# The queries' row factor: from two TensorE transposes a pair to a block turn on VectorE and a way through DRAM

## The chip, the cores and the metric

The kernel runs on one core of one Trainium2 chip. The metric is the device time of one execution in microseconds. TensorE (PE, with its weight loads PEld), VectorE (DVE), ScalarE (ACT), GpSimd (POOL) and SyncE (SP) each run their own queue of instructions and wait for one another through semaphores.

## The reference

128 sequences of 128 tokens, 256 hidden numbers, 16 heads of 16. A gated cross-attention with an additive bias, then a gated mixture of 8 experts of which each token takes one:

```python
x = x + tanh(g_xattn) * attention(layernorm(x), ctx, ctx, bias, Wq.., Wk.., Wv..)   # LoRA merged into W
x = x + tanh(g_ffn) * ffn(layernorm(x))       # argmax over 8 experts, gelu, two 256x256 products
# attention: scores = (q * D**-0.5) @ k.T + bias; softmax; out = p @ v
# layernorm(x) = (x - mean) / sqrt(var + 1e-5), one mean and one factor for each row (token)
```

## The kernel before

The attention half runs in steps, one for each sequence: in step k TensorE multiplies the scores of sequence k, while earlier and later sequences stand at other stages (`seq(i, k, lag)` gives the sequence that is lag steps back; a negative lag is ahead). Eight steps make one round of a hardware loop on each engine. The order inside a step is written out by hand for each engine. Queries and keys are projected for two sequences at once: in an even step the queries of a pair (`qry`, two sequences ahead), in an odd step its keys (`ky`, one ahead). The expert half follows; the change does not touch it.

The layernorm of the queries is folded into the projection: the weights are centred, so that only the factor 1/sqrt(var+eps) of each token is missing. It is a column: one number on each of 128 partitions, in `ln[:, row, 0, 0]`, made by GpSimd (L486) five steps ahead of the sequence's scores. The projected queries lie with the hidden numbers on the partitions and the tokens along the free axis, so the factor is needed as a row, the same on all partitions: `RS`, 128 x 256 for a pair.

One even step on TensorE runs thus (the lines are those of the profile): scores of k (L575), for which it waits that x2T of the step before was read (L638), scaled_ok and others; the values product of k-2 (L609); the first eight transposes of the scores of k-1 (L600); four transposes of the output (L676); then the two transposes of the row factor (L707), each with `ln`'s column broadcast along the free axis, into the unused half of bank 6; the query projection (L625, eight matmuls); the value projection (L735) into the other half of bank 6, after a wait that ScalarE has copied the row factor out; two transposes of the normalised rows (L749) into bank 3; the last eight transposes of the scores of k-1 (L600). Then the next step's scores, which overwrite banks 0 to 3. An odd step has the key projection in place of the query projection and no row factor. Every fourth step adds the expert logits (L648, L679), the next one the count sums (L685, L686).

ScalarE in a step: copy of the logits (L885, every fourth step), copy of the output (L870), two exponentials (L876), the second layernorm (L863), in an even step the copy of the row factor out of PSUM (L910), in an odd step the key activations (L853), the copy of V (L917), the copy x2T (L923), two more exponentials (L876), in an even step the bias activations of the queries (L842). VectorE: in every fourth step the picking of experts (L1063 to L1076), in the next the list of slots; 16 additions of the bias with their maximum (L1035); the division by the softmax sums (L1130, L1134), the residual (L1141), in an even step `scale_queries` (L1094), which multiplies the projected queries in PSUM by RS, the statistics for the layernorms (L1045, L1050, L1058). GpSimd subtracts the maxima (L462), makes the factors (L484, L486, L491), adds the value bias (L499) and scatters the normalised rows to DRAM (L519). SyncE issues all loads of the steps; ScalarE's queue issues DMAs only before the steps (weights, L830, L832) and after them (L332).

Of the kernel before, what the change touches and what calls it, by code (L numbers as in the profile page):

```python
# [12 lines left out]
P = 128  # L13
# [85 lines left out]
def flamingo_block(nc, x, x_turned, ctx_in, bias, wqT, wkT, wvT, bv, lora_in,  # L99
                   w1, w2, b2, consts, out):  # L100
    ctx = ExitStack()
    with ctx:
        def sb(name, shape, dt=F32):
            return ctx.enter_context(nc.sbuf_tensor(name, shape, dt))

        def sem(name):
            return ctx.enter_context(nc.semaphore(name))

        rows_dram = nc.dram_tensor("rows_dram", (DUMMY + FT, ROW), F32, kind="Internal").ap()

# [24 lines left out]
        sc = sb("sc", [P, 4, HEADS * P])  # L135
        RS = sb("RS", [P, 2 * P])
        XT = sb("XT", [P, 2, KC, 2 * P])
# [62 lines left out]
        b_x, b_o = bank[6], bank[7]  # L200
        b_v, b_rs, b_x2 = b_x[:, 0:HID], b_x[:, HID:HID + 2 * P], b_s[3]
        o_ps = b_o[:].rearrange("p (h c) -> p h c", c=CELL)
# [49 lines left out]
        xT_in = [sem(f"xT_in{i}") for i in range(2)]  # L252
        rs_ready, rs_evac = sem("rs_ready"), sem("rs_evac")
        s_setc, scaled_ok = sem("s_setc"), sem("scaled_ok")
# [287 lines left out]
        def _(pe):  # L542
# [86 lines left out]
            def step(i, k):  # L629
# [69 lines left out]
                if isinstance(i, int) and k in (N - 2, N - 1):  # L699
                    turn_rows(early[k - N + 2])  # L700
                if qry and qry.slot(2) == 0:
                    pe.wait_ge(rs_ok, qry.n(1, 2))
                    if not cur and val.reached(1):
                        pe.wait_ge(v_evac, val.n())
                    for n in range(2):
                        rs = ln[:, (qry.k + n - 7) % 8, 0, 0:1].broadcast_to([P, P])
                        ins = nc.tensor.transpose(b_rs[:, P * n:P * n + P], rs, ident)  # L707
                    ins.then_inc(rs_ready, 1)
                if cur and (qry or ky):
# [17 lines left out]
                if val:  # L727
                    pair, tok = val.k // 2 % 4, P * val.slot(2)
                    pe.wait_ge(ctx_inn[pair], val.per(8, 16, 16))
                    if qry and qry.slot(2) == 0:  # L730
                        pe.wait_ge(rs_evac, qry.per(2, 1, 1))
                    elif not cur and val.reached(1):
                        pe.wait_ge(v_evac, val.n())
                    for c in range(KC):
                        ins = mm(b_v, CT[:, pair, c, tok:tok + P], W["v"][:, c, :],  # L735
                                 start=(c == 0), stop=(c == KC - 1))
                    ins.then_inc(v_ready, 1)
# [90 lines left out]
        def _(act):  # L828
# [43 lines left out]
            def probs(t, q):  # L872
                act.wait_ge(tr_ready, t.n(4, q + 1))
                if q == 0 and t.reached(2):
                    act.wait_ge(ot_ready, t.n(1, -1))
                nc.scalar.activation(PT[:, t.slot(2), 512 * q:512 * q + 512], turn_bank(t, q)[:],  # L876
                                     ACT.Exp).then_inc(pt_ready, 1)

            def step(i, k):
                val, qry, ky, prev, fin, old, gate = (seq(i, k, lag) for lag in (-3, -2, -1, 1, 2, 3, 4))  # L880
                if gate and gate.slot(4) == 3:
                    act.wait_ge(lt_ready, gate.per(4, 1, 1))
                    if gate.reached(4):
                        act.wait_ge(l_ok, gate.per(4))
                    nc.scalar.copy(LT[:], b_lt).then_inc(lt_evac, 1)  # L885
# [20 lines left out]
                if isinstance(i, int) and k in (N - 2, N - 1):  # L906
                    copy_rows(early[k - N + 2])
                if qry and qry.slot(2) == 0:
                    act.wait_ge(rs_ready, qry.per(2, 1, 1))
                    nc.scalar.copy(RS[:], b_rs).then_inc(rs_evac, 1)  # L910
                if ky and ky.slot(2) == 0:
                    keys(ky)
                if val:
                    act.wait_ge(v_ready, val.n(1, 1))
                    if val.reached(8):
                        act.wait_ge(ot_ready, val.n(1, -7))
                    nc.scalar.copy(V[:, val.slot(8), :, 0:D],  # L917
                                   b_v.rearrange("p (h d) -> p h d", d=D)).then_inc(v_evac, 1)
                if old:
                    act.wait_ge(x2t_ready, old.n(1, 1))  # L920
# [7 lines left out]
                if qry and qry.slot(2) == 0:  # L928
                    queries(qry)

            early = [At(0, k, FU) for k in range(5)]
# [50 lines left out]
        def _(dve):  # L982
# [106 lines left out]
            def scale_queries(t):  # L1089
                pair = t.k // 2 % 2  # L1090
                dve.wait_ge(rs_evac, t.per(2, 1, 1))
                for o in range(KC):
                    dve.wait_ge(q_ready, t.per(2, KC, o + 1))
                    ins = nc.vector.tensor_tensor(QT[:, pair, o, :], b_s[o][:, 0:2 * P], RS[:], ALU.mult)  # L1094
                ins.then_inc(scaled_ok, 1)

            def step(i, k):
                cur, done, gate, ahead = seq(i, k, 0), seq(i, k, 2), seq(i, k, 4), seq(i, k, -5)
                qry = seq(i, k, -2)
                grp, was_grp = seq(i, k, 5), seq(i, k, 6)  # L1100
# [9 lines left out]
                if cur:  # L1110
                    for q in range(4):
                        add_bias(cur, q)
                if here.reached(2) and (gate or done or grp):
                    dve.wait_ge(o_ready, here.n(1, -1))
# [281 lines left out]
```

## Time and profile before

| | us |
|---|---|
| median of 3 runs (lowest, highest) | 1283.41 (1283.16, 1283.64) |
| the profiled execution | 1286.07 |
| its span | 1284.2 |
| attention steps | about the first 970 of the span |

Shares of busy time over the whole span, and the span in 40 slices (each digit the busy share in tenths; the last quarter is the expert half):

```profile
PE 1250.6 (97%) x12696; PEld 1071.5 (83%) x12696; DVE 996.9 (78%) x5961; ACT 781.1 (61%) x1724; POOL 999.9 (78%) x1051
PE   8999999999999999999999999999998799999997
DVE  6778888888888888888888888887897556555654
ACT  2767667677767676777676767776676333333332
POOL 3778889889888888888888888888888544554545
PEclk9999999999999999999999999999999899999999
```

TensorE's matmuls are pipelined, so the time of one in the trace is longer than what it holds of TensorE. A wait of an engine stands in brackets behind the instruction that ended it.

### The profile page before, as it was taken

What the parts mean: (1) busy time and instruction counts of PE and PEld (TensorE: products, weight loads), DVE (VectorE), ACT (ScalarE), POOL (GpSimd) and SP (SyncE); (2) the same over time, 40 slices, a digit from 0 to 9 for tenths busy, and PEclk for the clock granted to TensorE, in tenths of its full rate; (3) what the DMA queues carried; (4) which work ended last, traced back from release to release, by engine and by line L of the source; (5) the groups of instructions that cost most, each with busy time, mean ns of one, the idle gap of its engine ahead of it and who ended that gap; (6) DMA issues with size and microseconds to landing.
All of it is one profiled execution on the core that took longest, in us unless ns stands there. A gap on an engine that the chain in (4) does not pass through costs nothing.

```text
span 1284.2 us, 45363 instructions
## 1 busy us (share of the span) xinstructions
PE 1250.6 (97%) x12696; PEld 1071.5 (83%) x12696; DVE 996.9 (78%) x5961; ACT 781.1 (61%) x1724; POOL 999.9 (78%) x1051
## 2 busy tenths in 40 slices
PE   8999999999999999999999999999998799999997
PEld 6888888888888888888888888887887678888886
DVE  6778888888888888888888888887897556555654
ACT  2767667677767676777676767776676333333332
POOL 3778889889888888888888888888888544554545
PEclk9999999999999999999999999999999899999999
DMA  7656666666666666666666666666666388988885
GB/s 261 221 192 219 215 203 208 207 210 213 201 207 217 212 202 213 209 213 201 209 221 206 210 206 219 203 201 198 204 201 217 120 251 275 283 278 274 284 268 181
DMA packets 119875, 280.34 MB, mean 218 GB/s; under 512 B 16356, under 2 KB 35302, under 8 KB 119680
## 3 DMA queue, kind: packets, MB, share of 16 engines
q1 hardware_dynamic: 106128, 243.55, 59.7%
q0 software_dynamic: 12624, 34.62, 6.9%
q10 hardware_dynamic: 1056, 1.39, 0.4%
q8 instruction: 28, 0.46, 0.2%
q14 instruction: 39, 0.32, 0.1%
HBM read 243.50 MB, written 36.91 MB: 218 GB/s over the span
## 4 chain that ended last, share of the span: by engine, by line
PE 90%; issue 3%; DVE 3%; DMA 1%; POOL 1%; another core or an unknown queue 1%; ACT 1%; POOLq 0%; DVEq 0%; ACTq 0%
PE bank L600 18%; PE bank L625 17%; PE bank L575 11%; PE bank L609 9%; PE bank L735 8%; PE bank L778 8%; PE bank L792 7%; PE bank L676 4%; PE bank L749 2%; PE bank L766 2%; DMA out<-og,ids 1%; PE bank L648 1%; PE bank L707 1%; DVE sc L1035 1%
## 5 line engine op out<-in xcount | busy, mean ns | idle before, releaser
L1035 DVE CUSTOM_DVE_ANT_0 sc<-bank,sc 128x128 f32<-128x128 f32 x2048 | 442.9, 286 | 121.6 <-PE bank L575 109.9
L462 POOL TENSOR_TENSOR sc<-sc,rowmax 128x1024 f32<-128x1024 f32 x256 | 480.3, 1900 | 21.0 <-DVE rowmax L1035 16.7
L876 ACT ACTIVATE PT<-bank 128x512 f32<-128x512 f32 x512 | 279.9, 603 | 2.5 <-PE bank L600 1.8
L600 PE MATMUL bank<-cst,sc 128*128 128x128 f32 x2048 | 272.6, 276 | 0.6 <-POOL sc L462 0.6
L600 PEld LDWEIGHTS bank<-cst,sc 128*128 128x128 f32 x2048 | 225.4, 140 | 26.6 <-issue 25.3
L534 POOL DMA_INDIRECT out<-og,ids x120 | 118.3, 986 | 120.4 <-issue 113.7
L519 POOL DMA_INDIRECT rows_dram<-x2n,slot_i x128 | 135.2, 1056 | 62.1 <-issue 55.8
L1035 DVE DVE_READ_ACCUMULATOR2_ANT rowmax<- 128x1 f32 x2048 | 170.1, 83 | 0.2 <-issue 0.2
L870 ACT COPY OT<-bank 128x512 f32<-128x512 f32 x128 | 75.0, 586 | 134.9 <-PE bank L609 134.9
L575 PE MATMUL bank<-KT,QT 32*128 32x256 f32 x2048 | 146.7, 400 | 3.4 <-ACT V L917 1.2
L609 PE MATMUL bank<-PT,V 128*32 128x128 f32 x4096 | 137.6, 275 | 0.6 <-ACT PT L876 0.6
L853 ACT ACTIVATE KT<-bank,bk_half,cst 128x256 f32<-128x256 f32 x256 | 123.6, 563 | 21.9 <-PE bank L625 20.7
L609 PEld LDWEIGHTS bank<-PT,V 128*32 128x32 f32 x4096 | 106.6, 110 | 32.4 <-ACT PT L876 27.2
L917 ACT COPY V<-bank 128x256 f32<-128x256 f32 x128 | 48.4, 378 | 138.7 <-PE bank L735 138.7
L735 PE MATMUL bank<-wv,CT 128*128 128x256 f32 x512 | 132.3, 381 | 0.0
L792 PE MATMUL bank<-CT,hT 128*128 128x256 f32 x516 | 124.5, 383 | 5.7 <-DVE sc L1257 5.7
L625 PE MATMUL bank<-XT,wq 128*128 128x256 f32 x512 | 124.7, 388 | 4.3 <-DVE rowmax L1035 4.3
L625 PE MATMUL bank<-CT,wk 128*128 128x256 f32 x512 | 123.7, 384 | 0.9 <-DVE rowmax L1035 0.9
L778 PE MATMUL bank<-xgT,w_sb 128*128 128x256 f32 (+1 forms) x552 | 123.0, 366 | 0.0
L575 PEld LDWEIGHTS bank<-KT,QT 32*128 32x128 f32 x2048 | 92.8, 184 | 28.8 <-issue 24.2
L792 PEld LDWEIGHTS bank<-CT,hT 128*128 128x128 f32 x516 | 98.1, 192 | 19.3 <-ACT hT L949 6.1
L735 PEld LDWEIGHTS bank<-wv,CT 128*128 128x128 f32 x512 | 98.0, 191 | 13.6
(151 smaller groups left out, 1964.4 us busy)
## 6 DMA issues: line engine op xcount, KB each, us to landing
sc<-in_bias SPq DMA_DIRECT2D x256, 512.0 KB
w_sb<-in_w SPq DMA_DIRECT2D x69, 257.0 KB
CT<-in_w SPq DMA_DIRECT2D x69, 256.0 KB
xg<-rows_dram SPq DMA_DIRECT2D x63, 272.0 KB
x_sb<-in_x SPq DMA_DIRECT2D x128, 128.0 KB, 2.0
CT<-in_ctx_in SPq DMA_DIRECT2D x64, 256.0 KB, 4.7
XT<-in_x_turned SPq DMA_DIRECT2D x64, 256.0 KB, 2.7
rows_dram<-x2n,slot_i POOLq DMA_INDIRECT x128
```

The lines of the kernel that those rows point to most:

```text
L462: nc.gpsimd.tensor_tensor(s, s, m, ALU.subtract).then_inc(sub_ok, 1)
L519: nc.gpsimd.indirect_dma_start(rows_dram, bass.IndirectOffsetOnAxis(ap=slot_i[:, g, j:j + 1], axis=0), x2n[:, t.slot(8), :], None).then_in ...
L575: ins = mm(b_s[j][:, 2 * P * c:2 * P * c + 2 * P], QT[rows, pair, c, P * sq:P * sq + P], KT[rows, pair, c, sq].rearrange("p e k -> p (e k) ...
L600: ins = nc.tensor.transpose(turn_bank(t, q)[:, P * h:P * h + P], sc[:, t.slot(4), o:o + P], ident)
L609: ins = mm(b_x[CELL * j:CELL * j + CELL, P * (h // 4):P * (h // 4) + P], V[:, t.slot(8), h, :], PT[:, t.slot(2), P * h:P * h + P], start=T ...
L625: ins = mm(b_s[o][:, 0:2 * P], W[w][:, c, o * P:o * P + P], moving[:, c, :], start=(c == 0), stop=(c == KC - 1))
L735: ins = mm(b_v, CT[:, pair, c, tok:tok + P], W["v"][:, c, :], start=(c == 0), stop=(c == KC - 1))
L778: ins = mm(h_bank(t)[:, FT * o:FT * o + P * halves(t)], w1_of(t)[:, c * HID + o * P:c * HID + o * P + P], xgT[:, t.slot(2), c, 0:P * halve ...
L792: ins = mm(y_half, hT[:, t.slot(2), c, a * P:a * P + P], w2_of(t)[:, c * HID:c * HID + HID], start=(c == 0), stop=(c == KC - 1))
L853: ins = nc.scalar.activation(KT[:, pair, o, :, e, :], b_s[o][:, 0:2 * P].rearrange("p (s k) -> p s k", s=2), ACT.Identity, bias=bk_half[:, ...
L876: nc.scalar.activation(PT[:, t.slot(2), 512 * q:512 * q + 512], turn_bank(t, q)[:], ACT.Exp).then_inc(pt_ready, 1)
L1035: ins = nc.vector.tensor_tensor_reduce(out=s, in0=b_s[q][:, P * (h % 4):P * (h % 4) + P], in1=s, scale=1.0, scalar=LOWEST, op0=ALU.add, op ...
```

## The change

TensorE no longer transposes the row factor, ScalarE no longer copies it out of PSUM, and neither waits for the other over it. In their place, for each sequence t in step t-4: VectorE turns `ln`'s column, broadcast to 32 columns, in blocks of 32x32, so that one partition of each strip of 32 holds the 32 factors of its strip as a row (behind the bias additions). ScalarE's queue sends these four rows of 32 numbers to DRAM, 512 bytes (behind the copy of V, ahead of the copy x2T), and at the end of the same step, after a wait that they have landed, loads them back, broadcast to 128 partitions, into RS. RS becomes two buffers, one for each pair in flight. `scale_queries` waits for the loads.

```diff
+        rs_dram = nc.dram_tensor("rs_dram", (N, STRIPS, STRIP), F32, kind="Internal").ap()
-        RS = sb("RS", [P, 2 * P])
+        RS, rs_turned = sb("RS", [P, 2, 2 * P]), sb("rs_turned", [P, 2, STRIP])
 # TensorE, step
-                if qry and qry.slot(2) == 0:
-                    pe.wait_ge(rs_ok, qry.n(1, 2))
-                    if not cur and val.reached(1):
-                        pe.wait_ge(v_evac, val.n())
-                    for n in range(2):
-                        rs = ln[:, (qry.k + n - 7) % 8, 0, 0:1].broadcast_to([P, P])
-                        ins = nc.tensor.transpose(b_rs[:, P * n:P * n + P], rs, ident)
-                    ins.then_inc(rs_ready, 1)
...
-                    if qry and qry.slot(2) == 0:
-                        pe.wait_ge(rs_evac, qry.per(2, 1, 1))
-                    elif not cur and val.reached(1):
+                    if not cur and val.reached(1):
                         pe.wait_ge(v_evac, val.n())
 # ScalarE
+            def send_scale(t):
+                act.wait_ge(rs_turn, t.n(1, 1))
+                act.nop(nofuse=True)
+                act.dma_start(rs_dram[t.n()], rs_turned[0:P:STRIP, t.slot(2), :]).then_inc(rs_out, 16)
+
+            def spread_scale(t):
+                pair, tok = t.k // 2 % 2, P * t.slot(2)
+                act.wait_ge(rs_out, t.n(16, 16))
+                act.nop(nofuse=True)
+                act.dma_start(RS[:, pair, tok:tok + P], rs_dram[t.n()].rearrange("(a b) c -> a (b c)", a=1)
+                              .partition_broadcast(P)).then_inc(rs_in[pair], 16)
 # ScalarE, step
+                behind = seq(i, k, -4)
-                if qry and qry.slot(2) == 0:
-                    act.wait_ge(rs_ready, qry.per(2, 1, 1))
-                    nc.scalar.copy(RS[:], b_rs).then_inc(rs_evac, 1)
                 if ky and ky.slot(2) == 0:
                     keys(ky)
                 if val:
...
                     nc.scalar.copy(V[:, val.slot(8), :, 0:D],
                                    b_v.rearrange("p (h d) -> p h d", d=D)).then_inc(v_evac, 1)
+                if behind:
+                    send_scale(behind)
                 if old:
                     act.wait_ge(x2t_ready, old.n(1, 1))
...
                 if qry and qry.slot(2) == 0:
                     queries(qry)
+                if behind:
+                    spread_scale(behind)
 # VectorE
             def scale_queries(t):
                 pair = t.k // 2 % 2
-                dve.wait_ge(rs_evac, t.per(2, 1, 1))
+                dve.wait_ge(rs_in[pair], t.per(4, 32, 32))
...
-                    ins = nc.vector.tensor_tensor(QT[:, pair, o, :], b_s[o][:, 0:2 * P], RS[:], ALU.mult)
+                    ins = nc.vector.tensor_tensor(QT[:, pair, o, :], b_s[o][:, 0:2 * P], RS[:, pair, :], ALU.mult)
+            def turn_scale(t):
+                dve.wait_ge(rs_ok, t.n(1, 1))
+                if t.reached(2):
+                    dve.wait_ge(rs_out, t.n(16, -16))
+                dve.nop(nofuse=True)
+                nc.vector.transpose(rs_turned[:, t.slot(2), :], ln[:, (t.k - 7) % 8, 0, 0:1].broadcast_to([P, STRIP])
+                                    ).then_inc(rs_turn, 1)
 # VectorE, step
                 if cur:
                     for q in range(4):
                         add_bias(cur, q)
+                if behind:
+                    turn_scale(behind)
                 if here.reached(2) and (gate or done or grp):
                     dve.wait_ge(o_ready, here.n(1, -1))
```

## Rows read from the trace of the kernel before

**Rows 1.** Busy time by engine, 60 to 960 us: window, length, busy (count), clock, DMA.
```profile
60.00:960.00 900.00, 895.47 (x10436) 765.75 (x10434) 762.56 (x5075) 630.62 (x1398) 790.81 (x823) 1.00 0.63 207
```

**Rows 2.** Chain that ended last, two even steps: start us, share us, what.
```profile
507.21 0.24 PE bank L707 x2
...
521.91 0.22 PE bank L707 x2
```

**Rows 3.** Instruction groups by form on VectorE: count, busy us, mean ns, idle before.
```profile
L1035 DVE DVE_READ_ACCUMULATOR2_ANT rowmax<- 128x1 f32 x2048 | 170.1, 83 | 0.2 <-issue 0.2
L1130 DVE RECIPROCAL rden<-bank 128x16 f32<-128x16 f32 x128 | 32.0, 250 | 1.0 <-PE bank L676 1.0
L1124 DVE TENSOR_TENSOR where<-bank,cst 128x32 f32<-128x32 f32 x32 | 6.0, 186 | 1.8 <-PE bank L686 1.4 <-PE bank L690 0.4
```

**Rows 4.** Timeline, end of an even step: start us, length us, engine, line, instruction.
```profile
524.75 0.37 ACT L917 COPY V<-bank 128x256 f32<-128x256 f32 x1 [1.85 <-PE bank L735]
525.02 0.38 ACT L923 COPY x2T<-bank 128x256 f32<-128x256 f32 x1
525.09 0.33 SPq L371 DMA_DIRECT2D XT<-in_x_turned  x1
525.74 0.50 PE L575 MATMUL bank<-KT,QT 32*128 32x256 f32 x4
```

**Rows 5.** Timeline, ends of two odd steps.
```profile
516.67 0.59 PE L735 MATMUL bank<-wv,CT 128*128 128x256 f32 x2
517.39 0.38 ACT L917 COPY V<-bank 128x256 f32<-128x256 f32 x1
517.64 0.41 ACT L923 COPY x2T<-bank 128x256 f32<-128x256 f32 x1
518.29 0.50 PE L575 MATMUL bank<-KT,QT 32*128 32x256 f32 x4
...
533.04 0.41 ACT L923 COPY x2T<-bank 128x256 f32<-128x256 f32 x1
533.63 0.71 PE L575 MATMUL bank<-KT,QT 32*128 32x256 f32 x8
```

**Rows 6.** Timeline, query scaling and next scores: expert-picking step; the one late step.
```profile
540.08 0.74 DVE L1094 TENSOR_TENSOR QT<-bank,RS 128x256 f32<-128x256 f32 x2
541.18 0.50 PE L575 MATMUL bank<-KT,QT 32*128 32x256 f32 x4
...
889.86 0.75 DVE L1094 TENSOR_TENSOR QT<-bank,RS 128x256 f32<-128x256 f32 x2
890.70 1.15 PE L575 MATMUL bank<-KT,QT 32*128 32x256 f32 x16 [0.64 <-issue]
```

**Rows 7.** Single lines, 520-526 and 517-519 us: count, ns min/median/max, start us.
```profile
L922 ACTq EVENT_SEMAPHORE  x1: 17/17/17, 524.8 to 524.8; - x1
...
L571 PEldq EVENT_SEMAPHORE  x1: 438/438/438, 517.7 to 517.7; - x1
```

**Rows 8.** Timeline, DMA issues on SyncE's and ScalarE's queues.
```profile
518.59 0.85 SPq L380 DMA_DIRECT2D sc<-in_bias  x2
...
1021.63 0.58 ACT L939 COPY xgT<-bank 128x512 f32<-128x512 f32 x1
1021.78 0.34 ACTq L332 DMA_DIRECT2D rows_dram<-vacant  x1
```

**Rows 9.** Timeline, the output copy that follows the even step of rows 4.
```profile
528.40 0.59 ACT L870 COPY OT<-bank 128x512 f32<-128x512 f32 x1 [0.54 <-PE bank L609]
```

**Rows 10.** DMA issues: count, KB each, median us from issue to landing.
```profile
x_sb<-in_x SPq DMA_DIRECT2D x128, 128.0 KB, 2.0
CT<-in_ctx_in SPq DMA_DIRECT2D x64, 256.0 KB, 4.7
```

**Rows 11.** Timeline, the start of the kernel.
```profile
12.69 0.37 ACT L917 COPY V<-bank 128x256 f32<-128x256 f32 x1 [7.79 <-PE bank L735]
...
14.97 0.85 DVE L1094 TENSOR_TENSOR QT<-bank,RS 128x256 f32<-128x256 f32 x2
```

More of the change, by code:

```diff
@@ L200, in flamingo_block @@
         b_x, b_o = bank[6], bank[7]
-        b_v, b_rs, b_x2 = b_x[:, 0:HID], b_x[:, HID:HID + 2 * P], b_s[3]
+        b_v, b_x2 = b_x[:, 0:HID], b_s[3]
         o_ps = b_o[:].rearrange("p (h c) -> p h c", c=CELL)
@@ L252, in flamingo_block @@
         xT_in = [sem(f"xT_in{i}") for i in range(2)]
-        rs_ready, rs_evac = sem("rs_ready"), sem("rs_evac")
+        rs_turn, rs_out, rs_in = sem("rs_turn"), sem("rs_out"), [sem(f"rs_in{i}") for i in range(2)]
         s_setc, scaled_ok = sem("s_setc"), sem("scaled_ok")
@@ L1090, in scale_queries @@
                 pair = t.k // 2 % 2
-                dve.wait_ge(rs_evac, t.per(2, 1, 1))
+                dve.wait_ge(rs_in[pair], t.per(4, 32, 32))
                 for o in range(KC):
                     dve.wait_ge(q_ready, t.per(2, KC, o + 1))
-                    ins = nc.vector.tensor_tensor(QT[:, pair, o, :], b_s[o][:, 0:2 * P], RS[:], ALU.mult)
+                    ins = nc.vector.tensor_tensor(QT[:, pair, o, :], b_s[o][:, 0:2 * P], RS[:, pair, :], ALU.mult)
                 ins.then_inc(scaled_ok, 1)
+            def turn_scale(t):
[5 more added lines that the diff above has]
+                                    ).then_inc(rs_turn, 1)
             def step(i, k):
                 cur, done, gate, ahead = seq(i, k, 0), seq(i, k, 2), seq(i, k, 4), seq(i, k, -5)
-                qry = seq(i, k, -2)
+                qry, behind = seq(i, k, -2), seq(i, k, -4)
                 grp, was_grp = seq(i, k, 5), seq(i, k, 6)
```

## Prediction

> **What bounds the kernel now.** I first took the busy times of the long stretch of attention steps: TensorE is busy for 895.5 of 900 us at the full clock, VectorE for 763, GpSimd for 791, ScalarE for 631 [rows 1]. Next I read the chain of work that ended last; in that stretch it runs through TensorE without a break. The pieces that the change removes stand on it as 0.22 and 0.24 us for the two transposes of one pair of sequences, between the transposes of the output and the query projection [rows 2]. I take 0.23 us a pair.
>
> Then I asked what may hold up TensorE if ScalarE gets later, because the change puts new work into ScalarE's queue. The timeline of an even step (queries) and of two odd steps (keys) answers that. At the end of a step TensorE does the value projection (L735), ScalarE copies it (V, L917), then copies the turned rows (x2T, L923), and the next step's scores (L575) wait for x2T (L638: x2T was read out of bank 3, which the scores overwrite). In the even step x2T ends at 525.40 and the scores start at 525.74; in the odd steps 518.05 and 518.29, 533.45 and 533.63 [rows 4, 5]. So x2T comes in 0.18 to 0.34 us ahead. Not all of this is spare, since a semaphore takes time: where VectorE was late once, its last operation ended at 890.61 and the scores started at 890.70, 0.09 us later [rows 6]. TensorE's own queue says the same: in the odd step its last wait before the scores took 438 ns from 517.7, so it ended about when x2T did [rows 7]. In the even step one more wait of that queue follows x2T's, by about 0.1 us (my estimate from the wait's 51 ns and the 0.34 us there). That leaves as spare about 0.15 us in an even step, 0.15 and 0.09 us in odd ones: some 0.54 us in four steps.
>
> **The change, part by part.**
>
> *The transposes, their waits and the copy out of PSUM go.* 64 pairs times 0.23 us is 14.7 us off TensorE's chain [rows 2]. The copy (L910) costs nothing and gives nothing: behind it ScalarE waits 1.85 us for the value projection [rows 4]. The wait for it ahead of the value projection ended long before.
>
> *The turn on VectorE,* one 128x32 operation in each of 128 steps, behind the bias additions. No transposition stands in the trace. The nearest row is a 128x32 addition of 186 ns; below it stands the accumulator's read-out of 83 ns, above it the 128x16 reciprocal of 250 [rows 3]. I take 0.19, the same shape. Its waits are for GpSimd's factor, made a step earlier, and for a DMA of two sequences before. Queued behind it are the division, the residual and scale_queries, for which the next scores wait. In the tightest step of four (expert picking) scale_queries ends at 540.82 and the scores start at 541.18 [rows 6], so 0.27 us is spare after the 0.09. Whether that is used up depends on the next item: if the scores get later by themselves, VectorE stays hidden.
>
> *The send on ScalarE,* in 128 steps, between V's copy and x2T's copy. This is the term that decides. It is a wait (turn done: met, since the turn follows the bias additions by over a microsecond), the address, and a DMA issue. The price of an issue with its address comes from SyncE's queue: two in 0.85 us, each 0.33, so 0.52 from one to the next; an issue on ScalarE's own queue took 0.34 [rows 8]. With the wait, 0.06 to 0.13, and the wait and push of x2T's copy, about 0.10 (estimates from the same spacing), x2T starts some 0.70 us after ScalarE's queue gets past V's copy. Today it starts 0.27 us after V's copy in the even step and 0.25 in the odd [rows 4, 5]. So x2T gets later by about 0.45 us in an even step. In odd steps the key activations keep V's copy waiting a little (the value matmuls end at 517.26, the copy starts at 517.39 [rows 5]), the queue gets past it 0.1 us earlier, and the delay is about 0.35.
>
> Can the queue pass V's copy while that copy still waits for TensorE? The trace says no: in the even step the wait ahead of x2T's copy (L922, for a semaphore long met) ran at 524.8, when V's copy started at 524.75, though ScalarE had been idle for 1.85 us [rows 4, 7]. The Trainium skill, "Perfetto Trace Analysis", section "DVE / Act Engine Instruction", says that the sequencer is ready for the next instruction as soon as the one before is pushed into the wait queue; by that the send would go out during the idle time and cost nothing. The row speaks against this when the pushed instruction still waits.
>
> Of the delay the spare comes off: even steps 0.45 - 0.15 = 0.30, odd steps 0.35 - 0.15 = 0.20 and 0.35 - 0.09 = 0.26, so 1.06 us in four steps. Steps in which a send stands ahead of such scores are 121, or 30 fours: 32 us. At a cheaper issue (0.29 instead of 0.35: every delay 0.1 less with its waits) it is 20 us; if ScalarE's issues meet SyncE's (one starts at 525.09, some 0.1 us after the send would [rows 4]), and each delay is 0.12 us more, 46 us.
>
> The exponentials behind x2T get later too, but the scores that follow get later by nearly the same, so the values product finds them as today.
>
> *The spread on ScalarE,* at the end of each step: it waits until the send has landed, then one issue, 0.6 us. Behind it are the copy of the logits and of the output (L870), which gates TensorE's transposes. Before the output copy that follows an even step ScalarE idles 0.54 us [rows 9], and while an activation executes the queue goes on (an issue at 1021.78 began 0.15 us into a copy [rows 8]), so the issue hides under the bias activations of the queries and in that idle time. The landing must come within about 2.7 us of the send's issue (a step's output copy starts about 3.3 us after V's copy, 528.40 against 524.75 less the logits' 0.3, and the issue takes 0.6). The nearest row is x_sb's load, 2.0 us for 128 KB; a load of 256 KB takes 4.7 [rows 10]. Half a kilobyte should not take longer than 128 KB. Cost: nothing, with bounds 0 and 0.3 us a step.
>
> *DMA traffic:* 64 KB a step more against about 1.6 MB (207 GB/s for 7.5 us); the DMA engines are at 0.63 [rows 1]. Nothing. *GpSimd:* its waits do not change, and it is 791 us busy where TensorE will not get faster in this forecast. Nothing.
>
> *The start.* scale_queries of the first pair ran at 14.97, V's first copy at 12.69 [rows 11]. The second sequence's send stands behind that copy: issue at about 13.3, landed (2.0 us) at 15.3, spread issued at 15.4 and landed at 17.4: 2.4 us later than today, and the first keys and scores stand behind it.
>
> **Sum.** -14.7 + 32 + 2.4 = +20 us (+8 to +34 by the bounds of the send). The profiled execution took 1286.1 us, its span 1284.2 with 1.9 around; the median of the runs is 1283.4, 2.7 below. So 1306 on the profiled one, 1304 us as a median, 1291 to 1318 with the bounds.
>
> **The rivals.**
>
> *A, faster: the send is free.* ScalarE's queue issues the DMA before V's copy starts, or fast enough to fit the spare. The 1.85 us of idle time speak for it, L922 against it. Then TensorE wins 14.7 and loses 2.4 at the start, but VectorE's chain decides in the tightest step: 0.23 (TensorE earlier) + 2 x 0.19 (two turns since VectorE last waited) - 0.27 = 0.34 us in four steps, 11 us in all. 1271 without that, about 1275 with it at the cheapest turn (0.12 us in four steps, 4 us), 1282 at the likeliest. The point from which it decides: a delay of x2T under 0.13 us. The page named above would put the send where this rival has it.
>
> *B, no change:* delays of 0.25 us; four steps lose 1.0 - 0.54 = 0.46 and win 0.46. 1284 to 1286.
>
> *C, much slower: the landing is late.* A write to DRAM that needs 3.0 us holds ScalarE at the spread for 0.3 us in each step, 36 us more: 1340. For it: the 4.7 us of the larger load [rows 10]. Against: the size. It decides above 2.7 us.
>
> *D, the transposes' time is not won,* since another engine was as near: 14.7 us more than forecast, 1318.
>
> **How the numbers follow.** Forecast 0.60, A 0.18, B 0.08, C 0.08, D 0.06. This kernel's measurement tells about 0.2%, 2.6 us, from no change: below 1280.8 is faster, above 1286.0 slower. A gives 0.12 faster and 0.06 within; B 0.05 within and 0.03 slower; the rest is slower. Faster 0.12, within 0.11, slower 0.77. The range takes in the send's bounds, D and most of B and A, and leaves out C and the fast half of A: 1277 to 1326.
>
> **What would show it.** In the timeline of the changed kernel an issue of 0.3 to 0.4 us stands on ScalarE's queue right behind each start of V's copy; x2T's copy starts 0.6 to 0.75 us after V's, not 0.27; TensorE idles 0.2 to 0.3 us before each first score matmul; the scores two steps apart, 15.44 us now (525.74 to 541.18 [rows 4, 6]), are 15.44 - 0.23 + 0.53 = 15.7 us apart; the query projection follows the output transposes at once; scale_queries ends well ahead. I am wrong if the issue stands before V's copy, if x2T starts as early as now, if ScalarE idles at the spread, or if the scores wait for scale_queries.

## The result: 56 us slower, where 20 were forecast

The changed kernel takes 1339.68 us (median of 4 runs, 1336.37 to 1341.89) against 1283.29 us before: a ratio of 1.0438, 95% interval 1.0416 to 1.046. The direction was forecast, the size was not: the time lies outside the predicted range of 1277 to 1326 us. The profiled execution took 1339.97 us, its span 1338.0 us, 53.8 more than before's 1284.2.

The first view is again the busy time between 60 and 960 us. Its columns are those of [rows 1]: the window, its length, the busy time (and count) of PE, PEld, DVE, ACT and POOL, the granted clock, the share of the DMA engines and GB/s. Two rows of the page follow it, the chain that ended last and the scores:

```profile
60.00:960.00 900.00, 850.26 (x9822) 723.72 (x9821) 735.83 (x4935) 588.79 (x1269) 751.93 (x785) 1.00 0.63 208
...
PE 77%; issue 6%; DMA 6%; ACT 4%; DVE 3%; ACTq 1%; POOL 1%; another core or an unknown queue 1%; DVEq 0%; POOLq 0%
...
L576 PE MATMUL bank<-KT,QT 32*128 32x256 f32 x2048 | 146.7, 399 | 45.8 <-issue 30.1
```

TensorE, busy for 895.5 of 900 us before, is now busy for 850.3. Over the whole run the scores alone have 45.8 us of idle time ahead of them, and the chain is no longer TensorE's throughout. No other engine became the bound: VectorE, GpSimd and ScalarE are all busy for less of the stretch than before.

Where the 53.8 us are was found by comparing when the scores of each of the 128 steps start in both traces:

| stretch | forecast, us | measured, us |
|---|---|---|
| up to the first scores (19.6 before, 30.7 after) | +2.4 | +11.1 |
| from there to step 114, 28.5 times four steps | 28.5 x (1.06 - 0.46) = +17 | 28.5 x 1.36 = +38.8 |
| the step at the loop's end (114 to 115) | 0 | +5.3 |
| the rest | 0 | -1.4 |
| sum | +20 | +53.8 |

The loop's row can be split further. I measured the time on TensorE from the start of one group of matmuls to the start of the next, as a mean over the steps between 480 and 860 us, and subtracted before from after. In four steps (even, odd, even, odd) the difference is -0.25 and -0.22 for the removed transposes (in the two even steps), +0.08 for one query projection, and +0.40, +0.39, +0.47 and +0.48 from the last score transposes to the next scores. Everything else agrees to 0.01. So the loss sits where the prediction put it, ahead of the scores, but it is 1.74 us in four steps and not 1.06. The timeline of an even and an odd step, which answers [rows 4, 5], tells why:

```profile
511.17 0.37 ACT L918 COPY V<-bank 128x256 f32<-128x256 f32 x1 [2.05 <-PE bank L726]
511.43 0.55 ACTq L873 DMA_DIRECT2D rs_dram<-rs_turned  x1
512.08 0.37 ACT L926 COPY x2T<-bank 128x256 f32<-128x256 f32 x1 [0.53 <-issue]
512.55 1.15 PE L576 MATMUL bank<-KT,QT 32*128 32x256 f32 x16 [0.32 <-issue]
...
518.94 0.38 ACT L918 COPY V<-bank 128x256 f32<-128x256 f32 x1
519.05 0.55 ACTq L873 DMA_DIRECT2D rs_dram<-rs_turned  x1
519.70 0.37 ACT L926 COPY x2T<-bank 128x256 f32<-128x256 f32 x1 [0.38 <-issue]
520.17 0.50 PE L576 MATMUL bank<-KT,QT 32*128 32x256 f32 x4 [0.32 <-issue]
```

The send's issue (L873) takes 0.55 us, where the prediction had 0.34. x2T starts 0.91 and 0.76 us behind V, where 0.60 to 0.75 was announced, and in both of these steps the scores follow 0.10 us after x2T's end: nothing is spare any more. Note the label: "issue" means that TensorE waits for nothing that the profile names. It is the wait for x2T.

The start answers [rows 11]:

```profile
12.68 0.37 ACT L918 COPY V<-bank 128x256 f32<-128x256 f32 x1 [7.77 <-PE bank L726]
12.74 0.54 ACTq L873 DMA_DIRECT2D rs_dram<-rs_turned  x1
...
18.76 0.33 ACTq L879 DMA_DIRECT2D RS<-rs_dram  x1
19.13 0.37 ACT L918 COPY V<-bank 128x256 f32<-128x256 f32 x1 [6.08 <-DMA rs_dram<-rs_turned]
...
24.32 0.76 DVE L1099 TENSOR_TENSOR QT<-bank,RS 128x256 f32<-128x256 f32 x2 [9.51 <-DMA RS<-rs_dram]
25.13 3.78 PE L626 MATMUL bank<-CT,wk 128*128 128x256 f32 x8 [9.25 <-DVE QT L1099]
```

The second sequence's send is issued at 12.74, and the spread, which waits for its landing, only at 18.76; it lands at 24.3. Between 0 and 20 us the DMA engines are at 0.83 with the first loads, and half a kilobyte takes 6 us until the spread can be issued. So scale_queries starts at 24.32 where it started at 14.97 [rows 11], 9.4 of the 11.1 us. The rest is TensorE's clock: after 9.25 us of idle time the granted clock is 0.50 (1.2 GHz, the lower of its two levels; 24.3 to 29.7 us), and the first key projection takes 3.78 us. Before, at 1.00, it took half of that:

```profile
16.06 1.89 PE L625 MATMUL bank<-CT,wk 128*128 128x256 f32 x8
```

Later, by the records of the DMA engines, the send's packets are through 1.37 us after its issue began (median of 128).

And the loop's end, in the timeline of VectorE and TensorE, with the granted clock of the stretch behind the stop (last column but two):

```profile
937.50 0.29 DVE L1040 CUSTOM_DVE_ANT_0 sc<-bank,sc 128x128 f32<-128x128 f32 x1 [5.19 <-issue]
938.98 3.77 PE L626 MATMUL bank<-XT,wq 128*128 128x256 f32 x8 [4.91 <-DVE rowmax L1040]
...
937.60:944.40 6.80, 5.42 (x13) 4.20 (x14) 5.54 (x38) 0.00 (x0) 4.04 (x4) 0.50 0.18 34
```

The same two engines and stretch before:

```profile
884.28 1.89 PE L625 MATMUL bank<-XT,wq 128*128 128x256 f32 x8
887.55 0.29 DVE L1035 CUSTOM_DVE_ANT_0 sc<-bank,sc 128x128 f32<-128x128 f32 x1 [3.16 <-issue]
...
887.60:894.40 6.80, 5.01 (x85) 4.27 (x86) 5.87 (x42) 3.55 (x8) 3.87 (x6) 1.00 0.43 124
```

VectorE stands still for 5.19 us in the middle of the bias additions, once, where the unrolled last steps begin. Before, it did so too, for 3.2 us, at another of these additions; around both stops the instruction queue moves two pieces of 8 KB. The stop is 2 us longer, the step 5.3 us. Before, the stop fell behind the query projection and cost TensorE 2.4 us of idle time. Now TensorE stands idle for 4.9 us ahead of that projection, and from 937.6 us on the granted clock is 0.50: the query and the value projection together take 2.7 us more, about half of the 5.3.

### The profile page after: what moved, and what is told of

Its sections match the earlier page's. It is cut to its first block, busy times and chain, and to the rows that moved or that the text cites. A ratio compares the mean times of both kernels' runs of the same rounds, so it can differ in the third digit from the quotient of the medians.

```text
span 1338.0 us, 46226 instructions
## 1 busy us (share of the span) xinstructions
PE 1249.8 (93%) x12568; PEld 1066.7 (80%) x12568; DVE 1010.7 (76%) x6089; ACT 770.4 (58%) x1660; POOL 999.8 (75%) x1051
## 4 chain that ended last, share of the span: by engine, by line
PE 77%; issue 6%; DMA 6%; ACT 4%; DVE 3%; ACTq 1%; POOL 1%; another core or an unknown queue 1%; DVEq 0%; POOLq 0%
PE bank L626 14%; PE bank L601 14%; PE bank L576 10%; PE bank L610 8%; PE bank L783 7%; PE bank L769 7%; PE bank L726 6%; DMA RS<-rs_dram 4%; PE bank L677 4%; ACT KT L844 3%; PE bank L757 2%; PE bank L740 1%; PE bank L649 1%; DMA rs_dram<-rs_turned 1%; ACTq L873 1%
## 5 line engine op out<-in xcount | busy, mean ns | idle before, releaser
L576 PE MATMUL bank<-KT,QT 32*128 32x256 f32 x2048 | 146.7, 399 | 45.8 <-issue 30.1
L576 PEld LDWEIGHTS bank<-KT,QT 32*128 32x128 f32 x2048 | 98.0, 184 | 73.9 <-issue 62.8
L626 PE MATMUL bank<-XT,wq 128*128 128x256 f32 x512 | 127.5, 393 | 10.2 <-DVE rowmax L1040 9.8
L626 PEld LDWEIGHTS bank<-XT,wq 128*128 128x128 f32 x512 | 94.8, 195 | 22.6 <-issue 7.9
```

What stands on the lines that cost most here:

```text
L576: ins = mm(b_s[j][:, 2 * P * c:2 * P * c + 2 * P], QT[rows, pair, c, P * sq:P * sq + P], KT[rows, pair, c, sq].rearrange("p e k -> p (e k) ...
L626: ins = mm(b_s[o][:, 0:2 * P], W[w][:, c, o * P:o * P + P], moving[:, c, :], start=(c == 0), stop=(c == KC - 1))
```

## The experiments

The theory after the first reading: the loop loses by the price of the send's issue ahead of x2T, the start by landings under the first loads, the loop's end by VectorE's own stop. The clock behind the last two was no part of it. The rival is C of the prediction, which gave just this time (1340 us): landings hold ScalarE in each step. The transposes' gain, the turn and the spread were still without a price of their own.

**The gain alone.** The three calls are taken out, RS is filled once:

```
-                if behind:
-                    send_scale(behind)          # and spread_scale, turn_scale
-                dve.wait_ge(rs_in[pair], t.per(4, 32, 32))
+                dve.wait_ge(rs_turn, 1)         # memset(RS, 1.0) at the start
```

> Left out of the computation: the rows' factor (RS is filled with ones once); with it the turn, the send and the spread go, and TensorE's transposes stay away. This is the gain of the change alone. Theory (the time that the transposes took is won whole, the loss is all on ScalarE): 64 x 0.23 = 14.7 us less than before, 1268 us (1265 to 1272). Rival D of the prediction (another engine was as near): 1280 to 1284. In between (1272 to 1280) VectorE's chain would be next in the tightest step.

Measured: 1274.64 us, ratio 0.9927 (0.9908 to 0.9947). Four steps take 29.85 us instead of 30.20: the transposes give 0.47, and 0.11 come back in the expert-picking step. Of these 0.09 are in the query projection, which now follows a bf16 matmul directly and whose second matmul comes 0.30 us behind its first instead of 0.22. The time lies where I had expected VectorE's chain to be next, but it is this and not a wait for VectorE. Rival D has no case beyond that. The gain is 10 us, not 14.7.

**No send; then the turn alone; then the spread alone.**

```
-                if behind:
-                    send_scale(behind)                         # no send
-                act.wait_ge(rs_out, t.n(16, 16))
-                act.nop(nofuse=True)
-                act.dma_start(RS[:, pair, tok:tok + P], rs_dram[t.n()].rearrange("(a b) c -> a (b c)", a=1)
+                act.dma_start(RS[:, pair, tok:tok + P], x_seq[t.n()][0:1, 0:P].rearrange("(a b) c -> a (b c)", a=1)
...
-                if behind:                                     # turn alone
-                    send_scale(behind)                         # and spread_scale
...
-                if behind:                                     # spread alone: as no send, and
-                    turn_scale(behind)
```

> Left out: the send; the spread reads a row of the input x instead of rs_dram and waits for nothing. Turn and spread stay as they are. Theory (the send between V's copy and x2T's copy is the loss, turn and spread hide): about the time of the run with the gain alone, 1268 to 1274 us, x2T again 0.25 to 0.3 us behind V. Rival (the spread's issue or its traffic holds ScalarE or the loads too, 0.1 to 0.3 us a step): 1281 to 1307.

> Left out: send, spread and so the rows' factor (RS is ones, as in the run with the gain alone); the turn on VectorE stays in each step. It splits what the run without a send lost against the run with the gain alone (1290.6 against 1274.6 us). Theory (the turn stands ahead of the chain to the query projection in the step with the expert picking, 0.32 us in four steps, 10 us; and it moves the point in VectorE's code where the stop at the loop's end falls, 5 us): 1287 to 1293 us. Rival (the spread's traffic and issues cost those 16 us): 1273 to 1277 us.

> Left out: turn and send; the spread reads a row of x, as in the run without a send, so the rows' factor is missing. The run with the turn alone lost nothing in the loop (29.81 us for four steps) and 4 us at the loop's end; the run with turn and spread took 30.17 us for four. Theory (the spread's transfers make GpSimd's scatter land late, GpSimd waits 16 us for it between 300 and 800 us, and VectorE behind GpSimd; the turn has no part in it): four steps 30.1 to 30.2 us, no longer stop at the loop's end, 1284 to 1288 us. Rival (only turn and spread together make VectorE late): four steps 29.85 us, 1273 to 1277 us.

Measured: without a send 1290.57 us (1.0055), the turn alone 1276.73 (0.9944), the spread alone 1289.97 (1.0058). Without a send x2T is back at 0.25 to 0.28 us behind V: the send was the whole delay. But the 16 us above the gain alone are nearly all the spread's, not the turn's as I had expected for the second of these runs: the spread alone costs 15.3 us, the turn alone 2.1. In the loop four steps take 29.81 us with the turn and 30.18 with the spread, 10 us in all; at the start the first scores come 4.4 us later with the spread alone than with the gain alone. The view that separates them is GpSimd's groups between 300 and 800 us (busy, mean ns, idle before and its releaser), the turn alone first, then the spread alone:

```profile
L486 POOL TENSOR_SCALAR ve<-mv 128x2 f32<-128x2 f32 x67 | 14.9, 222 | 5.8 <-issue 0.2
```

```profile
L485 POOL TENSOR_SCALAR ve<-mv 128x2 f32<-128x2 f32 x66 | 14.6, 222 | 18.3 <-DMA rows_dram<-x2n,slot_i 14.1 <-issue 0.2
```

With the spread GpSimd waits 14.1 us for its own scatter to land, so its subtractions start later. By the DMA records the scatter is through 3.9 us after its issue with the spread and 3.0 with the turn (medians). VectorE pays for that in the expert-picking step, as the timeline of the run without a send shows:

```profile
591.81 3.75 POOL L463 TENSOR_TENSOR sc<-sc,rowmax 128x1024 f32<-128x1024 f32 x2
...
593.49 2.13 DVE L1061 TENSOR_TENSOR best<-L,lmax 128x32 f32<-128x32 f32 x1
...
598.37 1.99 PE L626 MATMUL bank<-XT,wq 128*128 128x256 f32 x8 [0.41 <-issue]
```

An operation of 128x32 elements takes 2.13 us, and ends 0.06 us after GpSimd's subtraction. In the picking steps of six traces the 0.06 is the same, with lengths from 1.36 to 2.13 us. Before, the operation was held too, for 1.45 to 1.50 us; the spread only moves the end of what holds it. The Trainium skill, "SBUF — State Buffer", section "SBUF: two separate sides", has the rule: VectorE with two SBUF inputs and a GpSimd operation that reads SBUF share a port pair; whichever starts first holds it for its whole instruction, and the other is blocked. The trace agrees. So the spread's traffic, costed at nothing, is worth 0.35 us in four steps in these two runs. In the changed kernel it is not paid: the scatter is through after 2.9 us there, and GpSimd does not wait for it. In these two runs the spread reads the input x and waits for no landing, so it comes at another time than in the change; what the change's own spread would cost beside a cheaper send is not shown by them.

**No spread, send kept.**

```
-                if behind:
-                    spread_scale(behind)      # RS is filled once; rs_out counted for each half of rs_turned
```

> Left out: the spread, so the rows' factor (RS is ones); turn and send stay in their places. Theory (the spread hides, as predicted, but for the start, where the waits for both landings go): four steps 31.5 us as in the changed kernel, the first scores 0 to 1 us late instead of 11: 1328 to 1332 us. Rival (the spread's wait and issue at the step's end take 0.1 us a step or more): below 1320 us.

Measured: 1321.48 us (1.0298). The first scores are 0.1 us late instead of 11.1, so the start's loss is the two landings. Four steps take 31.39 us instead of 31.56: in the changed kernel the spread costs at most 0.04 us a step, within its bounds, and rival C has no case; the landings do not hold ScalarE in the loop. The time lies between the two that were expected; the difference to 1328 us is this and a shorter stop at the loop's end (4.3 us, the step 2.1 us shorter).

**The price of the send's issue.**

```
-                act.dma_start(rs_dram[t.n()], rs_turned[0:P:STRIP, t.slot(2), :])
+                act.dma_start(rs_dram[t.n()], rs_turned[0:4, t.slot(2), :])
```

> The send takes partitions 0 to 3 of the turned tile instead of 0, 32, 64 and 96 (so it sends 32 of the 128 factors four times over); sizes, place and waits stay. It asks what the 0.55 us of the send's issue hang on, where the prediction had 0.34. If the partition step makes it dear: issue 0.35, x2T 0.2 us earlier in each step, 4 x 0.2 = 0.8 us in four steps, 31 fours: 25 us less than the changed kernel, 1315 us. If the issue costs 0.55 whatever the step: no difference, 1337 to 1342.

Measured: 1310.46 us (1.0196).

```profile
509.95 0.37 ACT L918 COPY V<-bank 128x256 f32<-128x256 f32 x1 [1.89 <-PE bank L726]
510.20 0.30 ACTq L873 DMA_DIRECT2D rs_dram<-rs_turned  x1
510.60 0.37 ACT L926 COPY x2T<-bank 128x256 f32<-128x256 f32 x1 [0.28 <-issue]
```

Four adjacent partitions take 0.30 us to issue, four that lie 32 apart 0.55. x2T starts 0.65 us behind V in even steps and 0.54 in odd ones. The four steps lose 0.15, 0.14, 0.14 and 0.22 ahead of the scores, 0.63 in all instead of 1.74, and take 30.45 us. Nothing but the partitions that are sent differs, so this is the disputed term by itself: 29 us.

**Another place for the send.** The call is moved behind `normalise(old)`, ahead of the keys.

```
                 if old:
                     normalise(old)
+                if behind:
+                    send_scale(behind)
...
-                if behind:
-                    send_scale(behind)        # between V's copy and x2T's
```

> The same work; the send stands on ScalarE's queue behind the layer norm's activation (L854) and ahead of the keys, where ScalarE has 0.5 to 1.2 us to wait for TensorE, instead of between V's copy and x2T's copy. Theory (only the place of the send costs, 0.64 and 0.54 us of delay of x2T a step): x2T is back at 0.25 to 0.3 us behind V, TensorE does not idle before the scores, the loop's four steps take 30.2 - 0.46 = 29.7 us, and what is left is the late start (11 us) and the stop at the loop's end (up to 5): 1277 to 1286 us. Rival (an issue on ScalarE's queue costs its 0.55 us wherever it stands, since the keys or V's copy get later): 1325 to 1342.

Measured: 1334.89 us (1.0395). The theory fell, though x2T is back at 0.25 us behind V. In even steps the send is free there (+0.03 us or less); in odd steps the keys take what x2T had:

```profile
528.60 0.21 DVE L1107 STREAM_TRANSPOSE rs_turned<-x2n 128x32 f32<-128x32 f32 x1
529.01 0.56 ACTq L873 DMA_DIRECT2D rs_dram<-rs_turned  x1
529.67 1.94 ACT L844 ACTIVATE KT<-bank,bk_half,cst 128x256 f32<-128x256 f32 x4 [0.94 <-PE bank L626]
531.48 0.38 ACT L920 COPY V<-bank 128x256 f32<-128x256 f32 x1
532.47 0.71 PE L576 MATMUL bank<-KT,QT 32*128 32x256 f32 x8 [0.57 <-ACT x2T L926]
```

The four key activations start 0.10 us after the issue's end, and V's and x2T's copies stand behind them. The label names TensorE's projection, but the sequencer was still at the issue. The odd steps lose 1.08 and 0.44 us. I had counted ScalarE's idle time ahead of V as room, and overlooked that in odd steps the keys fill it.

**The first pair by transposes as before.** The turns, sends and spreads begin with row 2.

```
-                if behind:
+                if behind and behind.reached(2):          # at turn, send and spread
...
+                if qry and not qry.reached(1):            # TensorE
+                    ins = nc.tensor.transpose(b_rs[:, P * n:P * n + P], rs, ident)
```

> The changed kernel, but the first pair of sequences gets its factors as before (two transposes and a copy); the turns, sends and spreads begin with the second pair. It asks what the start costs. In the changed kernel the first scores come 11.0 us late, since the first pair's send and spread each take 5 to 6 us to land under the first loads. Theory (the start costs that by itself, nothing else is moved): 1340 - 10 = 1330 us (1326 to 1333), four steps of the loop again 31.5 us. Rival (the second pair's send and spread are as late and hold the next scores): 1335 to 1340.

Measured: 1326.11 us (1.0333). Of the 11.1 us at the start 4.3 stay, since the second pair meets the same loads:

```profile
16.08 0.64 ACTq L884 DMA_DIRECT2D rs_dram<-rs_turned  x1
...
21.28 0.33 ACTq L890 DMA_DIRECT2D RS<-rs_dram  x1
21.66 0.56 ACT L855 ACTIVATE KT<-bank,bk_half,cst 128x256 f32<-128x256 f32 x1 [3.93 <-DMA rs_dram<-rs_turned]
```

The other gain came unasked: four steps take 31.20 us instead of 31.56. With other constants in its waits the sequencer has one register operation less there: the send's issue begins 0.18 (even) and 0.03 us (odd) behind V's start instead of 0.25 and 0.11, and x2T 0.89 and 0.68 us instead of 0.92 and 0.80.

**SyncE's queue.** Send and spread go to SyncE, each behind its own wait, ahead of the load of x; nothing new is on ScalarE, the first pair is as before. In the first run the column of factors is sent as it stands, 128 times 4 bytes, without a turn; in the second the turned tile, as in the change.

```
+                if behind and behind.reached(2):          # SyncE, ahead of the load of x
+                    sp.wait_ge(rs_ok, behind.n(1, 1))     # second run: rs_turn
+                    sp.dma_start(rs_dram[...], ln[:, (behind.k - 7) % 8, 0, 0:1]).then_inc(rs_out, 16)
+                    sp.wait_ge(rs_out, behind.n(16, -16))
+                    sp.dma_start(RS[...], rs_dram[behind.n()]...).then_inc(rs_in[...], 16)
```

> The whole computation. The column of factors goes to DRAM as it stands, 128 times 4 bytes, from SyncE's queue, where it waits for GpSimd's factor, and the spread follows there; no turn on VectorE, nothing new on ScalarE; the first pair as before by transposes. Theory (the loss was ScalarE's send and VectorE's turn, TensorE's gain is real): as the run with the gain alone, four steps 29.85 us instead of 30.20, no late start, no longer stop at the loop's end: 1270 to 1279 us. Rival (SyncE's wait for the landing makes the loads of x, the queries' input or the bias late): 1285 to 1310 us.

> The whole computation. As the run with the column on SyncE's queue (2049 us, its send landed some 10 us after its issue), but what is sent is the turned tile, 4 partitions of 128 bytes as in the change. Theory (what made it slow is the queue: the send and the spread stand behind the loads that SyncE issued before): send and spread again land 5 to 10 us after their issues, over 1700 us. Rival (128 pieces of 4 bytes were slow by themselves): landed after 1.4 us, 1285 to 1310 us.

Measured: 2049.26 us (1.5984) and 1393.6 us (1.0862). SyncE's queue in the one and in the other:

```profile
801.53 0.79 SPq L367 DMA_DIRECT2D rs_dram<-x2n  x1
...
811.73 0.33 SPq L371 DMA_DIRECT2D RS<-rs_dram  x1
```

```profile
506.27 0.56 SPq L367 DMA_DIRECT2D rs_dram<-rs_turned  x1
...
509.53 0.34 SPq L371 DMA_DIRECT2D RS<-rs_dram  x1
```

From the send's issue to the spread's, which waits for the landing, it is 10.6 us for the column and 4.7 for the turned tile (medians of 126; the latter from 1.7 to 8.2), against 1.37 us until the same half kilobyte is through on ScalarE's queue. Neither theory holds alone: behind the loads on SyncE's queue a landing takes some 3 us longer, with pieces of 4 bytes 6 more. (On ScalarE's queue the spread is issued 1.95 us after the send, median.) The Trainium skill, "DMA: Bandwidth & Descriptors", section "Issuing engines are not separate DMA queues", says that issuing from several engines only saves the sequencers' time; here the same send landed 3 us sooner on a queue without loads. What makes the column's kernel slow is loads of x that come late. Between 300 and 800 us of the column's run VectorE waits (total us, times, longest):

```profile
DVE st L1057 <- DMA x_sb<-in_x: 225.0, 36, 8.5
```

In the run with the turned tile the same wait is 33.1 us, and GpSimd's wait for its own scatter, 71.3 us, is the longest. So the rival of the first of these runs had the mechanism, late loads, and not its size. Part of the 2049 us is the clock: TensorE idles again and again, and the granted clock is 0.84 on average between 300 and 800 us.

**A cheaper form of the same work.** The whole turned tile is sent, which lies in adjacent partitions; in the second run once for each pair, in odd steps, with the first pair by transposes.

```
-                act.dma_start(rs_dram[t.n()], rs_turned[0:P:STRIP, t.slot(2), :])
+                act.dma_start(rs_dram[t.n()], rs_turned[:, t.slot(2), :])
...
-     rs_dram[t.n()].rearrange("(a b) c -> a (b c)", a=1).partition_broadcast(P)
+     rs_dram[t.n(), 0:P:STRIP, :].partition_broadcast(P)
```

> The whole computation, the change's own order. The send takes the whole turned tile (128 adjacent partitions, 128 bytes each) instead of partitions 0, 32, 64 and 96, and the spread reads rows 0, 32, 64 and 96 of it. Theory (the issue costs 0.55 us because the partitions lie apart; with adjacent ones it took 0.30): issue 0.30 to 0.36 us, x2T 0.2 us earlier than in the changed kernel, 1308 to 1320 us. Rival (the issue grows with the number of partitions sent, 128 instead of 4): issue 0.55 us or more, 1340 us or more.

> The whole computation. One send and one spread for each pair of sequences, in the odd steps, of the whole turned tiles; the first pair by transposes as before. Theory (each issue between V's copy and x2T's costs by itself; in the odd steps the cheap one cost TensorE 0.14 and 0.21 us): -0.38 + 0.34 = 0 us in four steps, 30.1 to 30.3; with 4 us at the loop's end and 2 to 4 at the start 1284 to 1292 us. Rival (the spread's transfers, as many bytes as before, make GpSimd's scatter late as in the run without a send, 0.3 us in four steps on top): 1293 to 1302 us.

Measured: 1353.93 us (1.0566) and 1598.7 us (1.2453). The issue did fall to 0.36 us, and x2T came 0.72 and 0.59 us behind V. But a spread that reads pieces of 128 bytes lands 6.0 us after its issue (by the profile's list of DMA issues), and one of a pair 9.9. The waits between 300 and 800 us, of the changed kernel, the whole tile and the pair (total us, times, longest):

```profile
DVE QT L1099 <- DMA RS<-rs_dram: 5.0, 5, 1.5
```

```profile
DVE QT L1099 <- DMA RS<-rs_dram: 32.9, 31, 1.6
```

```profile
DVE QT L1116 <- DMA RS<-rs_dram: 97.2, 25, 5.5
```

So the spread's landing has a limit too: the second row's spread is issued at the end of one step and needed by scale_queries in the next. At 4.8 us (the changed kernel, median from the DMA records) it is just met; at 6.0 us scale_queries waits in each even step, and in every second one the scores get 1.0 us later than before; with the send of four adjacent partitions the same step lost 0.14. In the pair's run the waits are longer, and behind them the granted clock falls: 0.915 on average over the run. The issue was forecast rightly, and both times were missed.

No version here that does the whole computation beats the kernel before. The most that the change could give is the gain alone, 0.7%; a spread beside it, as in the runs without a send, takes that back.

## Why the prediction was wrong, point by point

- **What bounds the kernel, and the spare.** Right. TensorE waits for x2T ahead of the scores; of the delay of x2T 0.63 us in four steps were spare, where 0.54 was worked out from [rows 4 to 7].
- **The transposes' gain.** 0.47 us in four steps on the spot, as forecast (0.46); 0.11 came back in the expert-picking step, most of it in the query projection: 10 us in place of 14.7.
- **The turn.** Hidden in the loop, as forecast, at 0.20 to 0.21 us (forecast 0.19). What was not forecast is the loop's end. In nine of the ten traces with the turn VectorE stops there for 4.2 to 6.2 us; in the four without it, before's among them, for 2.7 to 3.2. The tenth speaks against the turn as the whole cause: with the turned tile on SyncE's queue it is 2.3 us. That VectorE waits for its instructions, and that the turn moves the point, fits the transfers on the instruction queue, but is only argued. That TensorE then works at a granted clock of 0.50 is shown, and makes up half of the 5.3 us.
- **The send.** This is the step that failed. The mechanism held, and with it rival A fell: the queue does not get past V's copy while that copy waits. Of the 127 issues that follow a copy of V 117 began 0.06 to 0.43 us after its start, though ScalarE had been idle ahead of it for 2.05 us in the even step shown and 7.77 us at the start; the other ten began 0.03 to 0.40 us ahead of it, all in steps where ScalarE was busy up to V. The turn had ended at least 1.2 us before each of these issues, so it is not what they waited for. x2T is late, the scores are late. The issue was priced at 0.34 us by the nearest row, ScalarE's own issue in [rows 8], and took 0.55. x2T's delays are 0.64, 0.54, 0.64 and 0.55 us, not 0.45 and 0.35: 0.19 us too small in each step, 0.69 us too small in four steps after the spare, about 20 us in the loop, of 34 that were missed in all (8.7 at the start, 5.3 at the loop's end). With an issue of 0.30 us the time is 1310 us, though the start and the loop's end stay as they are. The bounds ("0.12 us more if issues meet") took their width from one shape of transfer, too; the row of [rows 8] moved another.
- **The spread.** Hidden on ScalarE, as forecast: in the loop all sends but one (3.3 us) are through within 2.7 us. That the spread's own landing has a limit, and that its traffic can delay GpSimd's scatter, was missing. In the changed kernel neither is paid for: the landing is just in time, and the scatter is not late.
- **The start.** The mechanism was right (the second send stands behind V's first copy), the size was off by 8.7 us: the landing of 2.0 us came from a median over the whole run [rows 10], and the first 25 us are not like the median. Of the 8.7 some 7 are the two landings, the rest is the clock that fell while TensorE stood idle, for which the forecast had no term.
- **Rival C** gave the measured time, 1340 us, by a mechanism that does not occur in the loop. A time that fits is no evidence for its cause.

## What to carry to other kernels

Price a DMA issue by a row of the same shape (partitions and their step), not by any row of the same engine: in an in-order queue it delays whatever stands behind it, unless that would have waited anyway. Price a landing by the stretch in which it happens, and give each transfer that something waits for its own deadline. Ask of each stop of TensorE what clock it works at afterwards. When a piece of work is moved to an engine that has idle time, look for what fills that time in the other kind of step.

## What the runs showed of the hardware that I had not expected

- An issue of four partitions of 128 bytes took 0.55 us with a step of 32 partitions and 0.30 us with a step of one; 128 adjacent partitions of 128 bytes took 0.36 us.
- The send of half a kilobyte was through after 1.37 us on ScalarE's queue; the spread that waits for it was issued 1.95 us after it there, 4.7 us on SyncE's queue among loads, and 5.2 to 6.1 us on ScalarE's queue during the first loads.
- After 9.25 us of idle time at the start and after 4.91 us at the loop's end TensorE's granted clock was 0.50 (1.2 GHz) for some microseconds, and eight projection matmuls took 3.8 us instead of 1.9; after the stop of the kernel before, with 1.72 and 0.64 us of idle time, it stayed at 1.00.
- One register operation less ahead of an issue that stands on the critical path came with 0.36 us less in four steps.
- In the run with the spread alone a transfer of 64 KB a step, with the DMA engines at 0.67, made another engine's scatter 0.9 us late, which shows as 14 us of waiting in 500; in the changed kernel, where the spread comes at another time, the scatter was not late.
